# Batch 0 of a Mamba and mixture-of-experts kernel: the side work of TensorE and ScalarE dealt anew over its sixteen steps

## The chip, the core and the metric

One NeuronCore of a Trainium2 chip runs the whole program. Its engines work from queues of their own and meet only at semaphores: TensorE (PE, with its weight loads as PEld), VectorE (DVE), ScalarE (ACT), GpSimd (POOL), and SyncE (SP), which here issues DMAs. The metric is the time of one execution on the device in microseconds, lower is better; the median of three runs of the kernel before is 659.77 us.

## What is computed

Eight sequences of 512 rows of 128 features go through a layer norm, and from its output through two branches that are added to x: a Mamba block and a mixture of 8 experts of which each row takes 2.

```python
xn = _layernorm(x)
# Mamba: 256 channels, 16 states
xn_ = xn * rsqrt(mean(xn * xn) + eps) * norm_w
x_s, z = split(xn_ @ in_proj_w.T)
u = silu(conv1d(x_s, conv_w, taps=4) + conv_b)
dt_raw, B, C = split(u @ x_proj_w.T)
delta = softplus(dt_raw @ dt_proj_w.T + dt_proj_b)
h_t = exp(delta_t * A) * h_(t-1) + delta_t * u_t * B_t     # for 16 states
y = (h * C).sum(states) + u * D_param
mamba = (y * silu(z)) @ out_proj_w.T + xn
# experts
top_w, sel = top_k(xn @ w_router.T, 2);  gates = softmax(top_w)
moe = sum_e gates[:, e] * ((silu(xn @ w_gate[e]) * (xn @ w_up[e])) @ w_down[e])
return x + mamba + moe
```

## The kernel before

The sequences are the batches 0 to 7 (`b`), the 16 states of the recurrence are the steps of a batch (`k`), and a batch has two halves `hf` of 128 channels. A step scans its state over all 512 positions at once: `scan` (L1070) on DVE, one instruction for each half, from the decay exp(delta A) and the input delta u B. Then `product` (L1087) multiplies the states with the row C, and PE adds it up over the steps in PSUM, transposed on the way (`accumulate`, L1354: eight 128x128 transposes). Each engine has a list of its own, written out by hand: `step0(k)` for the steps of batch 0, `step(b, k)` for those of the others, and which side work goes into which step stands in small tables. Nothing reorders it.

In batch 0 the input of the scan is not made by POOL, which is still busy with the norm, but by ScalarE and PE. `scaled(k)` (L518) scales the transposed delta u with the column B on ScalarE into `dbu`, four instructions; `dbu_turn(0, k, hf)` (L1317) turns it back into a PSUM bank, four transposes for each half. Three banks take turns, so the turn for half m waits until the product two halves before is done (`freed`, `p_rdy`). ScalarE also writes the decays (`decay`, L490) two steps ahead. From batch 1 on POOL makes the input (`scaled`, L883, two 128x512 products a step), and the decays are written into the PSUM bank (`decay_bank`, L502).

Beside this batch 0 carries side work:
- **Turned rows and logits.** `rows_normed` (L996, DVE, tensor_scalar from `x_sb` to `xh_all`, four for each group) makes the normed rows, the last two groups in steps of `LATE_ROWS`. `xh_turn(b)` (L1271) turns them on PE, `xh_out(b)` (L461) copies them to `xhT` on ScalarE, `logits(b)` (L1277) is the router's product, four matmuls 8 columns wide.
- **Choices.** When all logits are there, `choices` (L1005 to L1014) picks two experts on DVE in twelve operations. POOL adds the choices (`sel`), PE counts them (`totals`, `ranking`), ScalarE copies (`totals_out`, `ranks_out`), POOL works out the slots (L836 to L855, signals `lohi_rdy`), and DVE's `one_hots` (L1034, L1035, L1037; two groups a step by `HOT_STEP` in steps 12 to 15) with PE's `inverse` (L1304) invert the map. POOL's L861 to L864 make `texp`, the expert of each tile, on one partition; SP waits for it to load weights. In step 15 DVE makes the gates (`weights`, L1020 to L1024).
- **Front of batches 1 and 2.** `conv(c, hf, taps)` (L1386, two matmuls of 512 columns for each tap in fp32 passes, two taps a step), `half_tanh` (L690, L693) on ScalarE and `unit` (L1101) on DVE make u; `rows(c)` (PE L1401, ScalarE L699) makes B, C and dt, which SP stores (`rows_out`) and loads spread over all partitions (`rows_in`, `out_rows_in`); `steps_mm` (L1409), `magnitudes`, `vanishing`, `rounded`, `corrected`, `logarithm` (ScalarE) and `raise_sum`, `correct`, `softplus`, `input_scale` (POOL, L415, L421, L436, L444, one 128x512 operation for each half) make delta and delta u.
- **z and skip.** `z_mm` (L1437) and `z_gate` (ScalarE L647, DVE L1184) in the steps of `z_step(0)`; `skip` (L1366) adds u D into the sum, in `SKIPPED0`.
- **keep** (L1263) is a matmul whose result nobody reads.

POOL's own list before the choices is the weights' scaling (L787 to L791), 32 tensor_scalars of the norm (L795) and eight additions x + xn (L809, 128x512). SP's list has `rows_out(1)` ahead of `out_rows_in(0, 3)`, the C rows that products 12 to 15 read.

## Time and profile before

| | us |
|---|---|
| median of 3 runs | 659.77 (659.0 to 662.25) |
| the profiled execution | 662.08 |
| its span, first to last instruction | 660.2 |
| DVE busy | 604.0 (91%) |
| PE busy / ScalarE / POOL | 565.8 / 423.4 / 502.6 |
| batch 0's steps on DVE | 35.57 to 137.08 |

The page gives the share of each engine; the shares are means over stages with different limits, so batch 0 is read for itself: the table of stretches for how busy DVE is, the list of waits for what it waits on, and the timelines of DVE, PE, ScalarE and POOL side by side. A timeline row gives the start, the time from the start of the first to the end of the last of its instructions, engine, line, operation, tiles, and in brackets the idle time before it with what ended it. Durations of matmuls include their latency; the distance between starts is what they hold PE for.

### The profile page before, as it was taken

Reading aid. Unit: us, or ns where it says so; the run is one execution under the profiler, and the core shown is the slowest. Engines: PE = TensorE matmul, PEld = TensorE weight load, DVE = VectorE, ACT = ScalarE, POOL = GpSimd, SP = SyncE. Lnnn points to the kernel's source line nnn. Section 1 sums busy time; section 2 is a strip of 40 time slices with the busy share of each in tenths; the row PEclk is TensorE's granted clock in tenths of the full one; section 3 lists DMA queues with packets and bytes.
Section 4 is the critical chain, followed back from the end, with each engine's and each line's share of the span. In section 5 each row is a group of like instructions: output and inputs, shape, how many; then the busy total and the mean of one; then the engine's idle time right before and its main releaser. Section 6 shows DMA issues by size and latency. Waiting matters only on the chain.

```text
span 660.2 us, 11497 instructions
## 1 busy us (share of the span) xinstructions
PE 565.8 (86%) x3582; PEld 437.6 (66%) x3582; DVE 604.0 (91%) x867; ACT 423.4 (64%) x839; POOL 502.6 (76%) x504
## 2 busy tenths in 40 slices
PE   5979889888898989999898989989897876779788
PEld 2368576646777777777777777777774554657654
DVE  6966979999999999999999999999998886979957
ACT  1694797137656766657656766657654689469681
POOL 5794059459898798978998798978878869748770
PEclk9868989979999999999999999999998997899979
DMA  7450321425786986888787886888743343223621
GB/s 228 152 181 0 106 91 64 136 72 190 256 264 227 288 268 226 270 272 293 253 256 238 250 294 233 263 274 295 267 146 144 108 163 124 80 80 108 188 65 32
DMA packets 59198, 122.90 MB, mean 186 GB/s; under 512 B 8314, under 2 KB 39426, under 8 KB 52098
## 3 DMA queue, kind: packets, MB, share of 16 engines
q1 hardware_dynamic: 53922, 112.39, 50.3%
q0 software_dynamic: 4496, 9.45, 5.3%
q8 instruction: 29, 0.48, 0.3%
q10 hardware_dynamic: 720, 0.33, 0.3%
q14 instruction: 31, 0.25, 0.1%
HBM read 112.70 MB, written 9.44 MB: 185 GB/s over the span
## 4 chain that ended last, share of the span: by engine, by line
PE 46%; DVE 21%; ACT 15%; issue 10%; POOL 6%; DMA 1%; DVEq 0%; ACTq 0%; POOLq 0%
DVE bank L1070 9%; PE bank L1480 6%; PE bank L1386 6%; PE bank L1354 6%; DVE h_sb L1087 5%; PE bank L1494 4%; ACT dbu L518 4%; POOL dbu L883 4%; PE bank L1488 4%; PE bank L1317 3%; ACT da L490 3%; PE bank L1409 2%; PE bank L1401 2%; PE bank L1455 2%; PE bank L1263 2%
## 5 line engine op out<-in xcount | busy, mean ns | idle before, releaser
L883 POOL TENSOR_TENSOR dbu<-du,xn_all 128x512 f32<-128x512 f32 x178 | 223.2, 1276 | 57.3 <-DVE bank L1070 57.0
L1070 DVE TENSOR_TENSOR_SCAN bank<-bank,dbu 128x512 f32<-128x512 f32 x176 | 214.8, 1224 | 3.9 <-ACT bank L502 3.9
L502 ACT ACTIVATE bank<-delta,a_sb 128x512 f32<-128x512 f32 x176 | 121.4, 691 | 108.2 <-DVE h_sb L1087 106.2
L1087 DVE TENSOR_TENSOR h_sb<-bank,xh_all 128x512 f32<-128x512 f32 x240 | 159.8, 680 | 1.2
L1354 PE MATMUL bank<-id_sb,h_sb 128*128 128x128 f32 x992 | 134.7, 281 | 12.4 <-DVE h_sb L1087 10.9
L1354 PEld LDWEIGHTS bank<-id_sb,h_sb 128*128 128x128 f32 x992 | 116.2, 146 | 26.3 <-DVE h_sb L1087 19.3
L1070 DVE TENSOR_TENSOR_SCAN bank<-da,bank 128x512 f32<-128x512 f32 x76 | 90.5, 1218 | 34.0 <-PE bank L1317 33.8
L1480 PEld LDWEIGHTS bank<-wd_sb,hid 117*128 117x128 f32 (+1 forms) x432 | 55.2, 191 | 54.4 <-DVE hid L1121 31.3
L1480 PE MATMUL bank<-wd_sb,hid 117*128 117x128 f32 (+1 forms) x432 | 64.1, 284 | 24.5 <-ACT xT L661 12.5
L870 POOL DMA_INDIRECT xs<-xn_rows,src x72 | 70.6, 981 | 11.3 <-issue 7.4
L1317 PE MATMUL bank<-id_sb,dbu 128*128 128x128 f32 x304 | 52.1, 299 | 30.8 <-ACT dbu L518 27.5
L1317 PEld LDWEIGHTS bank<-id_sb,dbu 128*128 128x128 f32 x304 | 38.9, 154 | 50.3 <-ACT dbu L518 32.5
L518 ACT ACTIVATE dbu<-du_t,bc_sb 128x256 f32<-128x256 f32 x152 | 64.4, 496 | 0.4 <-PE bank L1317 0.3
L1488 PE MATMUL bank<-xT,wgu_sb 128*118 128x128 f32 x432 | 59.8, 275 | 4.1 <-DVE ga L1114 4.1
L1386 PE MATMUL bank<-xhT,wk_sb 128*128 128x512 f32 x128 | 61.4, 608 | 0.7 <-ACT xhT L461 0.7
L1494 PE MATMUL bank<-xT,wgu_sb 128*118 128x128 f32 x432 | 59.1, 272 | 0.0
L1488 PEld LDWEIGHTS bank<-xT,wgu_sb 128*118 128x118 f32 x432 | 52.3, 182 | 6.2 <-issue 6.1
L912 POOL DMA_INDIRECT xhT<-y_slots,slot x48 | 46.6, 971 | 12.1 <-issue 10.5
L490 ACT ACTIVATE da<-delta,a_sb 128x512 f32<-128x512 f32 x80 | 53.1, 711 | 2.9 <-DVE bank L1070 2.7
L1494 PEld LDWEIGHTS bank<-xT,wgu_sb 128*118 128x118 f32 x432 | 52.7, 182 | 0.5 <-issue 0.5
L667 ACT ACTIVATE th<-bank 118x384 f32<-118x384 f32 x72 | 34.7, 483 | 18.4 <-PE bank L1488 18.4
L1263 PE MATMUL bank<-wk_sb,id_sb 128*128 128x256 f32 (+3 forms) x108 | 46.3, 520 | 0.0
...
## 6 DMA issues: line engine op xcount, KB each, us to landing
xh_all<-b_rows SPq DMA_DIRECT2D x30, 1024.0 KB, 6.5
xn_all<-b_rows SPq DMA_DIRECT2D x25, 1024.0 KB, 7.3
...
```

Of the source, the lines that this page charges most:

```text
L490: nc.scalar.activation(da_of(n)[:, hf, :], delta[b % 2][:, hf, :], ACT.Exp, scale=a_sb[:, hf, k:k + 1]).then_inc(s["da_rdy"], 1)
L502: nc.scalar.activation(bank_of(b, m)[:, :], delta[b % 2][:, hf, :], ACT.Exp, scale=a_sb[:, hf, k:k + 1]).then_inc(s["da_rdy"], 1)
L518: last = nc.scalar.activation(dbuT[k % 2][:, t, :], duT[:, t, :], ACT.Copy, scale=bc_sb[q][:, t, k:k + 1])
L883: nc.gpsimd.tensor_tensor(dbu[k % 2][:, hf, :], du[b % 2][:, hf, :], b_ring[c % 2][:, k % CH, :], ALU.mult).then_inc(s["dbu_p"], 1)
L1070: nc.vector.tensor_tensor_scan(at, da_of(n)[:, hf, :] if n in IN_SBUF else at, inp, 0.0, ALU.mult, ALU.add).then_inc(s["h_rdy"], 1)
L1087: nc.vector.tensor_tensor(h_sb[k % 2][:, hf, :], bank_of(b, 2 * k + hf)[:, :], row, ALU.mult).then_inc(s["p_rdy"], 1)
L1317: last = nc.tensor.transpose(at[:, t * P:(t + 1) * P], dbuT[k % 2][:, t, hf * P:(hf + 1) * P], id_sb[:, :])
L1354: last = MM(HT[i][:, t % 2, hf * P:(hf + 1) * P], h_sb[k % 2][:, hf, t * P:(t + 1) * P], id_sb[:, :], is_transpose=True, start=(k == 0 and ...
L1386: last = MM(at[:, :], wk_sb[:, tap, hf * P:(hf + 1) * P], xhT[:, c, tap:tap + T], start=(tap == taps[0] if c == 0 else tap == 0), stop=(ta ...
L1480: last = MM(XD[:, P:P + H], hid[j % 2][0:FN[c], c * P:(c + 1) * P], wd_sb[j % NW][0:FN[c], c, :], start=(c == 0), stop=(c == NF - 1))
L1488: last = MM(GB[0:FW, c * P:(c + 1) * P], wgu_sb[j % NW][:, c * FS:c * FS + FW], xT[j % 2][:, :], start=True, stop=True)
L1494: last = MM(UB[0:FW, c * P:(c + 1) * P], wgu_sb[j % NW][:, F + c * FS:F + c * FS + FW], xT[j % 2][:, :], start=True, stop=True)
```

## The change

Only batch 0 and what leads to it are changed, and no operation of the reference. All row numbers here are of the kernel before.

PE: logits 1 and 2 go ahead of step 0 with three keeps; the other turns and logits go to the even steps 0 to 6 and 8. The conv of batch 1's second half goes to steps 3 and 5, batch 2's to 7, 8 and 13, 14. `totals` and `ranking` come in step 9, `rows(1)` in step 10, `steps_mm` in 11 and 12. Keeps stand in steps 0, 1, 12 and 15 alone. ScalarE copies turned rows one step after PE turned them, `rows(1)` comes in step 11, the magnitudes in 12 and 13, the logarithm in 13, `half_tanh(2, 1)` in step 15 behind `decay_bank`. DVE: late rows in steps 0 and 2, choices in step 8, units in 1, 6, 9 and 15. POOL: the eight operations of batch 1's front come last. Waits of conv and rows are changed to fit.

```diff
-    TURNED, SKIPPED, SKIPPED0 = 11, (1, 2), (7, 8)
+    TURNED, SKIPPED, SKIPPED0 = 11, (1, 2), (8, 10)
-        LOGITS_AT = {0: (1, 2), 1: (3,), 2: (4,), 3: (5,), 5: (6,), 6: (7,)}
-        LATE_ROWS = {0: (24, 28), 4: (28, 32)}
+        LOGITS_AT = {0: 3, 2: 4, 4: 5, 6: 6, 8: 7}
+        LATE_ROWS = {0: (24, 28), 2: (28, 32)}
...
-            return {0: 4, 2: 5, 3: 6, 5: 7}.get(k)
+            return {0: 4, 2: 5, 4: 6, 6: 7}.get(k)
...
-            return {13: 1, 15: 0} if b == 0 else {8: 1, 10: 0} if b == 6 else {4: 1, 6: 0}
+            return {12: 1, 14: 0} if b == 0 else {8: 1, 10: 0} if b == 6 else {4: 1, 6: 0}
...
+                if k == 10:
+                    ranks_out()
...
-                if b_turn(k) is not None:
-                    xh_out(b_turn(k))
-                if k in (0, 4):
-                    half_tanh(1, k // 4)
-                if k == 6:
+                if b_turn(k - 1) is not None:
+                    xh_out(b_turn(k - 1))
+                if k in (0, 6):
+                    half_tanh(1, k // 6)
+                if k == 9:
+                    half_tanh(2, 0)
+                    totals_out()
+                if k == 10:
+                    spread_choices()
+                if k == 11:
                     rows(1)
...
+                if k == 15:
+                    half_tanh(2, 1)
...
-                if k == 7:
+                if k == 8:
                     choices()
-                if k in (11, 14):
-                    unit(2, k // 14)
+                if k in (9, 15):
+                    unit(2, k // 15)
...
-                if k < 6:
+                if k < 2:
                     keep(LGB[:, 2 * C - 2 * H + 2 * E:])
-                if k >= 12:
+                if k == 12 or k == 15:
                     keep(MAP[:, P:], k == 12)
                     keep(MAP[:, P:], False)
```

On PE, steps 2 and 3 of batch 0, from the first turn of step 2's second half (each `L1317` row is one half, `L1354` the accumulation). Before:

```order
L1317 MATMUL bank<-id_sb,dbu 128x128 x4
L1354 MATMUL bank<-id_sb,h_sb 128x128 x8
L1317 MATMUL bank<-id_sb,dbu 128x128 x4
L1386 MATMUL bank<-xhT,wk_sb 128x512 x2
L1271 MATMUL bank<-id_sb,xh_all 128x128 x4
L1277 MATMUL bank<-wr_sb,xhT 128x8 x4
L1263 MATMUL bank<-wk_sb,id_sb 128x240
```

And now (step 2, then step 3; a conv pair is now L1388):

```order
L1317 MATMUL bank<-id_sb,dbu 128x128 x4
L1354 MATMUL bank<-id_sb,h_sb 128x128 x8
L1317 MATMUL bank<-id_sb,dbu 128x128 x4
L1277 MATMUL bank<-wr_sb,xhT 128x8 x4
L1271 MATMUL bank<-id_sb,xh_all 128x128 x4
L1317 MATMUL bank<-id_sb,dbu 128x128 x4
L1354 MATMUL bank<-id_sb,h_sb 128x128 x8
L1317 MATMUL bank<-id_sb,dbu 128x128 x4
L1388 MATMUL bank<-xhT,wk_sb 128x512 x2
```

A step's side work is now either a turn with logits or a conv pair, and the keep is gone.

On POOL, from the last operations of the slots to the first products of batch 1 (L421 corrects, L436 makes delta, L444 delta u, L415 raises the sum). Before:

```order
L855 CAST hi<-hi 128x64
L421 TENSOR_TENSOR sp_m<-sp_m,sp_e 128x512 x2
L436 TENSOR_TENSOR delta<-sp_d,sp_m 128x512 x2
L444 TENSOR_TENSOR du<-delta,u_sb 128x512 x2
L861 TENSOR_SCALAR wgu_sb<-lanes_sb,ends 1x72 x8
L822 TENSOR_TENSOR wgu_sb<-wgu_sb 1x288
L823 TENSOR_TENSOR wgu_sb<-wgu_sb 1x144
L824 TENSOR_TENSOR tsum<-wgu_sb 1x72
L864 TENSOR_SCALAR texp<-tsum 1x72
L883 TENSOR_TENSOR dbu<-du,xn_all 128x512 x6
```

And now:

```order
L856 CAST hi<-hi 128x64
L858 TENSOR_SCALAR wgu_sb<-lanes_sb,ends 1x72 x8
L825 TENSOR_TENSOR wgu_sb<-wgu_sb 1x288
L826 TENSOR_TENSOR wgu_sb<-wgu_sb 1x144
L827 TENSOR_TENSOR tsum<-wgu_sb 1x72
L861 TENSOR_SCALAR texp<-tsum 1x72
L415 TENSOR_TENSOR sp_m<-sp_m,sp_y 128x512 x2
L421 TENSOR_TENSOR sp_m<-sp_m,sp_e 128x512 x2
L436 TENSOR_TENSOR delta<-sp_d,sp_m 128x512 x2
L444 TENSOR_TENSOR du<-delta,u_sb 128x512 x2
L883 TENSOR_TENSOR dbu<-du,xn_all 128x512 x6
```

The eight 128x512 operations of batch 1's front stand in one row behind `texp`; the two raises stood ahead of the slots before.

On ScalarE, the end of step 14 and step 15 of batch 0 (with the semaphores waited for). Before:

```order
L690 ACTIVATE u_sb<-bank,cbh_sb 128x512 [waits p_rdy,xc_mm]
L693 ACTIVATE u_sb<-u_sb,sign_sb 128x512 [waits x_th]
L647 ACTIVATE zs_sb<-bank 128x512 [waits z_mm]
L502 ACTIVATE bank<-delta,a_sb 128x512 [waits delta_rdy,p_rdy] x2
L655 ACTIVATE g_sb<-bank 128x512 [waits acc_mm] x2
```

And now (the first row ends step 14):

```order
L650 ACTIVATE zs_sb<-bank 128x512 [waits z_mm]
L502 ACTIVATE bank<-delta,a_sb 128x512 [waits delta_rdy,p_rdy]
L693 ACTIVATE u_sb<-bank,cbh_sb 128x512 [waits p_rdy,xc_mm]
L696 ACTIVATE u_sb<-u_sb,sign_sb 128x512 [waits x_th]
L502 ACTIVATE bank<-delta,a_sb 128x512 [waits delta_rdy,p_rdy]
L658 ACTIVATE g_sb<-bank 128x512 [waits acc_mm] x2
```

The two instructions of `half_tanh(2, 1)` stand behind the first `decay_bank` of batch 1.

## Rows read from the trace of the kernel before

**Rows 1.** Stretches: from:to, length; busy us of each engine, PEclk, DMA, GB/s

```profile
35.57:137.08 101.51, 85.73 (x470) 66.84 (x470) 84.69 (x122) 66.69 (x127) 55.99 (x76) 0.86 0.28 96
...
160.00:300.00 140.00, 125.99 (x932) 106.10 (x933) 138.83 (x193) 90.86 (x184) 122.99 (x106) 1.00 0.77 254
```

**Rows 2.** Waits of DVE in batch 0: who, on whom, us in total, times, longest

```profile
DVE bank L1070 <- PE bank L1317: 15.8, 9, 4.7
```

**Rows 3.** Timeline of DVE: start, us, line, operation, [idle before]

```profile
47.27 1.23 DVE L1070 TENSOR_TENSOR_SCAN bank<-da,bank 128x512 f32<-128x512 f32 x1 [4.69 <-PE bank L1317]
...
66.70 1.11 DVE L996 TENSOR_SCALAR xh_all<-x_sb,mean,both 128x128 f32<-128x128 f32 x4
...
76.22 2.33 DVE L1070 TENSOR_TENSOR_SCAN bank<-da,bank 128x512 f32<-128x512 f32 x2
78.46 1.27 DVE L1087 TENSOR_TENSOR h_sb<-bank,u_sb 128x512 f32<-128x512 f32 x2
79.64 0.42 DVE L1005 COPY wgu_sb<-bank 128x256 f32<-128x256 f32 x1
```

**Rows 4.** Timeline of PE: own work, side work at two levels of the clock

```profile
40.12 1.12 PE L1317 MATMUL bank<-id_sb,dbu 128*128 128x128 f32 x4 [4.78 <-ACT dbu L518]
...
48.66 1.06 PE L1317 MATMUL bank<-id_sb,dbu 128*128 128x128 f32 x4
...
57.17 0.96 PE L1277 MATMUL bank<-wr_sb,xhT 128*128 128x8 f32 x8
...
60.22 1.88 PE L1386 MATMUL bank<-xhT,wk_sb 128*128 128x512 f32 x4
...
69.56 1.91 PE L1401 MATMUL bank<-u_sb,xp_sb 128*40 128x512 f32 x4
...
140.18 3.45 PE L1401 MATMUL bank<-u_sb,xp_sb 128*40 128x512 f32 x4
```

**Rows 5.** Stretches of one microsecond, the granted clock third from the end

```profile
38.00:39.00 1.00, 0.00 (x0) 0.00 (x0) 1.00 (x3) 0.97 (x3) 1.00 (x2) 0.50 0.78 238
...
54.00:55.00 1.00, 1.00 (x8) 1.00 (x7) 1.00 (x3) 0.00 (x0) 1.00 (x2) 0.72 0.00 0
```

**Rows 6.** Timeline of ScalarE: second half of a half_tanh, first decays of batch 1

```profile
102.71 0.72 ACT L693 ACTIVATE u_sb<-u_sb,sign_sb 128x512 f32<-128x512 f32 x1
...
131.06 1.30 ACT L502 ACTIVATE bank<-delta,a_sb 128x512 f32<-128x512 f32 x2 [7.80 <-DVE h_sb L1087]
```

**Rows 7.** Timeline of DVE: one-hots and gates beside POOL and alone

```profile
107.55 2.68 DVE L1034 TENSOR_TENSOR lo_oh<-lanes_sb,lo 128x1024 f16<-128x1024 f16 x1
...
132.13 0.94 DVE L1020 TENSOR_SCALAR p<-p 128x32 f32<-128x32 f32 x1
...
133.71 0.18 DVE L1023 TENSOR_SCALAR p<-p 128x32 f32<-128x32 f32 x1
...
134.14 0.69 DVE L1034 TENSOR_TENSOR lo_oh<-lanes_sb,lo 128x1024 f16<-128x1024 f16 x1
```

**Rows 8.** Timeline of POOL: seven of the eight additions

```profile
48.25 8.64 POOL L809 TENSOR_TENSOR x_sb<-x_sb,xn_all 128x512 f32<-128x512 f32 x7
```

**Rows 9.** Timeline of POOL and of DVE in the first 10 us

```profile
7.12 2.77 POOL L790 TENSOR_TENSOR wk_sb<-wk_sb,g_sb 128x256 f32<-128x256 f32 x4
...
7.29 0.58 DVE L984 TENSOR_SCALAR mean<-mean 128x4 f32<-128x4 f32 x1
...
9.27 0.65 DVE L989 TENSOR_SCALAR both<-both 128x8 f32<-128x8 f32 x1
```

**Rows 10.** Timeline of POOL: start of the slots, last of the front, end of the counts

```profile
92.20 0.20 POOL L836 TENSOR_SCALAR tiles<-wgu_sb 128x8 f32<-128x8 f32 x1 [3.27 <-ACT wgu_sb L471]
...
107.16 2.52 POOL L444 TENSOR_TENSOR du<-delta,u_sb 128x512 f32<-128x512 f32 x2
...
119.00 0.71 POOL L864 TENSOR_SCALAR texp<-tsum 1x72 int32<-1x72 f32 x1
```

**Rows 11.** DMA issues of the page: KB each, median us from issue to landing

```profile
xh_all<-b_rows SPq DMA_DIRECT2D x30, 1024.0 KB, 6.5
```

More of the change, by code:

```diff
@@ L829, in _ @@
             nc.gpsimd.tensor_tensor(kk[:, :], kk[:, :], irms[:, :], ALU.mult).then_inc(s["top_rdy"], 1)
-            for hf in range(NH):
-                raise_sum(pool, nc.gpsimd, 1, hf)
             pool.wait_ge(s["rk_out"], 1)
@@ L1505, in step0 @@
                     inverse(g)
-                if k in (2, 3):
-                    conv(1, 1, (2 * k - 4, 2 * k - 3))
-                if k == 5:
-                    rows(1)
+                if k == 9:
+                    totals()
+                    ranking()
+                if k in LOGITS_AT:
+                    logits(LOGITS_AT[k])
+                if b_turn(k) is not None:
+                    xh_turn(b_turn(k))
+                if k in (3, 5):
+                    conv(1, 1, (k - 3, k - 2))
+                if k in (7, 8):
+                    conv(2, 0, (2 * k - 14, 2 * k - 13))
+                if k == 10:
+                    rows(1)
+                if k in (11, 12):
+                    steps_mm(1, k - 11)
+                if k in (13, 14):
+                    conv(2, 1, (2 * k - 26, 2 * k - 25))
+                if k + 1 in z_step(0):
+                    z_mm(0, k)
                 if k in SKIPPED0:
                     skip(0, (SKIPPED0.index(k),))
-                if k == 8:
-                    totals()
-                    ranking()
-                if k in (9, 10):
-                    conv(2, 0, (2 * k - 18, 2 * k - 17))
-                if k in (12, 13):
-                    conv(2, 1, (2 * k - 24, 2 * k - 23))
-                if k + 1 in z_step(0):
-                    z_mm(0, k)
-                if b_turn(k) is not None:
-                    xh_turn(b_turn(k))
-                for i in LOGITS_AT.get(k, ()):
-                    logits(i)
-                if k == 7:
-                    steps_mm(1, 0)
-                    steps_mm(1, 1)
-                if k < 6:
+                if k < 2:
                     keep(LGB[:, 2 * C - 2 * H + 2 * E:])
-                if k >= 12:
+                if k == 12 or k == 15:
                     keep(MAP[:, P:], k == 12)
@@ L1615, in _ @@
             input_turn(0, 0)
+            logits(1)
+            keep(LGB[:, 2 * C - 2 * H + 2 * E:])
+            logits(2)
+            keep(LGB[:, 2 * C - 2 * H + 2 * E:])
+            keep(LGB[:, 2 * C - 2 * H + 2 * E:])
             for k in range(S):
```

35 lines of the change are left out of this document (15 added, 20 removed).

## Prediction, made before the changed kernel ran

> **What bounds the kernel now.** I read the table of stretches first. In batch 0's sixteen steps, 35.57 to 137.08 us, DVE is busy 84.69 of 101.51 us, and in 160 to 300 us 138.83 of 140 [rows 1]. So behind batch 0 DVE is full: whatever batch 0 ends earlier or later comes out at the end of the kernel nearly whole. The list of waits says what DVE's idle time in batch 0 is: 15.8 us in nine waits of scans on the transposes of `dbu_turn` (L1317) [rows 2], and 0.3 us on ScalarE at the start, which stays. DVE's timeline shows the pattern: at 47.27 a scan had waited 4.69 us; from 76.22 on nothing waits, and a full step is 2.24 us from scans to products and 1.18 us of products, 3.42 us in all [rows 3].
>
> The waits stand where PE's side work is longer than DVE's step. At full clock PE's own part of a step is about 1.8 us: each half of `dbu_turn` 0.44, `accumulate` 0.9. Two taps of `conv` add 1.72, one `logits` 0.82 [rows 4], `xh_turn` is as long as a half of `dbu_turn`, `keep` 0.5. Steps 2 and 3 now carry conv, turn, logits and keep together, 5.3 us. At the lower level all of it doubles: the transposes at 48.66 take 0.85 to the next start, and `rows` takes 3.4 us at 140.18 against 1.85 at 69.56 [rows 4]. PE had stood idle for 4.78 us before 40.12 [rows 4]; the granted clock is half from 38 us and rises at 54.7 [rows 5].
>
> **What the change takes away.** Odd steps now have a conv pair (1.8 + 1.7 = 3.5 us), even steps a turn and a logits (3.1 us): both about DVE's 3.42. Walking the steps with these lengths, scans of steps 2 to 9 find their transposes ready if the clock is high. What stays of the waits:
> - Step 1. Its first transposes are released by ScalarE's scaling at 40.12 as before; high clock leaves 0.5 us of the wait. The second half comes behind a logits, a turn and a keep: 0.95 us wait at 2.4 GHz, 2.65 at 1.2. PE's idle time shrinks from 4.78 to about 1.6 us, since logits 1 and 2 and three keeps (3.1 us) now fill it. I take the middle, 1.8.
> - Step 11. Step 10 has `rows` (1.85) and one skip (0.9) beside 1.8: 4.5 us, 0.1 us wait at the high level. But PE idles some 3 us while DVE makes the choices (twelve operations of DVE from 79.64, 5.37 us [rows 3]), and low clock makes rows 3.4 us: 2 to 3.5 us. Taken 2.6.
> - Step 15, a new wait. `unit(2,1)` now stands behind product 15, and its input is made by ScalarE behind `decay_bank(16,0)`, which itself waits for product(15,0). Decay 0.61 after 0.71, tanh 0.70, half 0.72: 2.77 us after that product's start [rows 6], while DVE is there after 1.18. Wait 1.6; the weights and the last one-hots queue behind it.
>
> Of 16.1 us idle, 0.3 + 0.5 + 1.8 + 2.6 + 1.6 = 6.8 stay: **-9.3 us**.
>
> **What it moves under POOL.** DVE operations with both inputs in SBUF, or tensor_scalar between SBUF tiles, get longer beside POOL's tensor_tensor. Two such places go: the one-hot at 107.55 took 2.68 us against 0.69 at 134.14, ending 0.58 behind POOL's last `du` product, and L1020 took 0.94 at 132.13 where its like at 133.71 took 0.18 [rows 7]. In the new order the count chain of 1-partition operations lies beside the first one-hots (-2.0), and POOL's product is over at L1020 (-0.75): **-2.75 us**.
>
> Two places come. First, `rows_normed(28, 32)` goes from step 4 (66.70, 1.11 us, POOL idle) [rows 3] to step 2, at 49 to 51 us, and POOL adds seven 128x512 tiles without a gap from 48.25 to 56.89 [rows 8]. How does DVE fare against such a chain? The early stretch shows tensor_scalars and tensor_tensors of a few elements against four back-to-back POOL products: each ends some 0.05 us after the POOL operation that it began in (7.29 takes 0.58, 9.27 takes 0.65, base 0.18; two more between them) [rows 9]. So one DVE operation per POOL operation: four at 0.6 + 3 x 1.2: **+4.2 us** (0.5 if all four slip through together, 6.6 if none until 56.89). PE then starves for 2.3 to 4 us; if the clock falls, the next two steps' side work (5.9 us against 3.42) costs 1.35 + 1.0. Between 0 and 2.35, taken **+1.5**.
>
> Second, the front of batch 1. Before, POOL's eight 128x512 operations were two by two: two raises at 86, then six from 102.18, the last two at 107.16 [rows 10], mostly beside scans and products that read PSUM. Now all eight come behind `texp`. Clock them from the end of the choices. DVE: steps 9 to 12 of 3.42, a unit 0.66, a z gate 0.6, the wait 2.6: first one-hots at 17.5; 2.94 long, then step 13: second pair at 23.9. POOL: sum of choices, totals, ranking, copy 4.6, slots 10.0 (from 92.20 to the chain of six), counts 10.1 (from that chain's end at 109.65 to the end of `texp`, 119.71) [rows 10]: the chain of eight starts at 24.7 and runs 8 x 1.25 = 10.0 us, to 34.7. It meets the second pair after about two of its six operations. The nearest row is the one-hot at 107.55: it waited past the end of one POOL product (108.4) to the end of the next, though it had asked 0.85 us before. If a gapless chain keeps it out, four operations (1.9 us, and 0.2 between) follow 34.7: 13.0 us for the pair against 3.8: **+9.2**. By one for one: 4 x 1.24, and 1.4 more in step 14's pair: +6.1. By slipping in once: +2.5. I take the row of the same operation, 9.2.
>
> The Trainium skill (SBUF — State Buffer, "Who interferes with whom") says that GpSimd and such a VectorE operation hold the pair of ports for one whole instruction. By that sentence alone the second term would be 6.1 and the time 659.5; the wait at 107.55 went past one instruction's end.
>
> **Costed at nothing.** The rows that product 12 reads (c_in, 1 MB) are now issued after ScalarE's rows(1) in step 11, not step 6; such a transfer lands 6.5 us after its issue in the median [rows 11], and 7 us of DVE work lie between. `lohi` is there at 14.6, asked at 17.5. `scaled(15)` waits for the logarithm and its table, over 9 us ahead of scan 15. POOL's product for batch 1 has some 10 us in hand without the stalls. `texp` and expert weights come earlier. Each wait that ends late would show as a DVE wait.
>
> **Sum.** -9.3 - 2.75 + 4.2 + 1.5 + 9.2 = **+2.85 us**. The profiled span of 660.2 would be 663.1 (its execution 662.08 would be 664.9, 1.9 us outside the span); on the median of 659.77, which is 2.3 below that execution, it gives **662.6**.
>
> **Rivals.**
> - One for one throughout: the HOT pair at +6.1, so -0.25: 659.5. For it: four early rows; against: 107.55.
> - DVE hardly kept out: rows 0.5, no clock loss, pair +2.5: -9.05, 650.7. For it: chains on POOL need not be as gapless once DVE asks; against: every row where both met.
> - Slower, one mechanism: POOL's chain of adds at 48.25 keeps `rows_normed` out until 56.89, 6.6 us, with the clock loss full, 2.35: +6.1, 665.9. It decides once the rows wait past the second POOL add.
> - Slower by the clock: two keeps instead of six in steps 0 to 5, so PE stays at 1.2 GHz through steps 2 to 8; each costs 1.9 to 2.8 us, so four such steps beyond the forecast give +9: 672.
> - The change does what it says and nothing is given back elsewhere: no row for it; it is the second rival.
>
> **How the numbers follow.** Chances: forecast 0.33, one for one 0.22, hardly kept out 0.2, adds keep it out 0.19, clock 0.06. The range takes in 650.7 with nothing below, and 665.9 with a microsecond of scatter: 650.5 to 667. A measurement tells apart about 0.5%, 3.3 us: faster means below 656.5, slower above 663.1. The second rival is faster, with some tail of the first: 0.24. Forecast (its centre just inside, split 0.17 same, 0.16 slower) and one for one (0.17 same, 0.02 slower): same 0.35; slower 0.41.
>
> **What would show it.** DVE's waits on L1317 in batch 0: about 5 us, none in steps 2 to 9 but one or two behind the rows. The four L996 near 50 us: 5 us in all if right, 1.1 if not, 7 if kept out. The third one-hot of L1034, some 24 us behind the choices: 9 to 10 us long, or split over L1034, L1035 and L1037 at 1.2 more each. A wait of 1.6 us before the L1101 of step 15. The lower clock at 78 to 88 us. If L996 and L1034 keep their lengths, the forecast is wrong by its two largest terms.

## The result, and the profile of the changed kernel

The changed kernel takes 663.11 us in the median of 20 runs (661.3 to 666.25), the kernel before 660.1 (658.04 to 662.75, 20 runs): a ratio of 1.0043, interval 1.003 to 1.0057. It is slower by a small step that is clear of noise. The profiled execution of the new kernel is its slowest, 666.25 us with a span of 664.5, and has the lowest mean granted clock of the twenty (0.943; the others 0.948 to 0.956), so its waits on PE may be longer than is typical; that of before had 662.08 us and a span of 660.2.

Line numbers on ScalarE, PE and GpSimd are shifted by a few (adds L809 are now L812, `half_tanh` L693 is L696, `conv` L1388); those of VectorE used here are the same. The first row answers to the first of [rows 1]: batch 0's steps, from the first scan to batch 1's.

```profile
35.40:138.67 103.27, 86.28 (x459) 68.74 (x459) 91.40 (x122) 65.18 (x124) 57.44 (x77) 0.81 0.27 94
```

Batch 0 got 1.76 us longer (101.51 before), and in it DVE is busy 6.7 us more with the same 122 instructions: the waits did go down, but operations got longer. The list of DVE's waits in that stretch (who, on whom, us in total, times, longest), beside [rows 2]:

```profile
DVE bank L1070 <- PE bank L1317: 9.0, 7, 2.9
DVE u_sb L1101 <- ACT u_sb L696: 1.5, 1, 1.5
DVE lo_oh L1034 <- PE bank L1304: 0.4, 1, 0.4
```

15.8 us in nine waits became 9.0 in seven, and two small ones are new. DVE's timeline shows where, and which operations got longer:

```profile
42.13 1.23 DVE L1070 TENSOR_TENSOR_SCAN bank<-da,bank 128x512 f32<-128x512 f32 x1 [2.10 <-PE bank L1317]
46.23 1.23 DVE L1070 TENSOR_TENSOR_SCAN bank<-da,bank 128x512 f32<-128x512 f32 x1 [2.88 <-PE bank L1317]
...
52.64 5.52 DVE L996 TENSOR_SCALAR xh_all<-x_sb,mean,both 128x128 f32<-128x128 f32 x4
58.08 2.33 DVE L1070 TENSOR_TENSOR_SCAN bank<-da,bank 128x512 f32<-128x512 f32 x2
...
68.19 1.23 DVE L1070 TENSOR_TENSOR_SCAN bank<-da,bank 128x512 f32<-128x512 f32 x1 [1.44 <-PE bank L1317]
...
98.07 1.23 DVE L1070 TENSOR_TENSOR_SCAN bank<-da,bank 128x512 f32<-128x512 f32 x1 [1.14 <-PE bank L1317]
...
104.84 0.68 DVE L1034 TENSOR_TENSOR lo_oh<-lanes_sb,lo 128x1024 f16<-128x1024 f16 x1
...
111.68 0.74 DVE L1034 TENSOR_TENSOR lo_oh<-lanes_sb,lo 128x1024 f16<-128x1024 f16 x1 [0.41 <-PE bank L1304]
112.34 1.52 DVE L1035 TENSOR_TENSOR hi_val<-lanes_sb,hi 128x576 f16<-128x576 f16 x1
113.90 1.41 DVE L1037 TENSOR_TENSOR hi_val<-hi_val,lanes_sb 128x576 f16<-128x576 f16 x1
115.24 1.76 DVE L1034 TENSOR_TENSOR lo_oh<-lanes_sb,lo 128x1024 f16<-128x1024 f16 x1
116.92 1.54 DVE L1035 TENSOR_TENSOR hi_val<-lanes_sb,hi 128x576 f16<-128x576 f16 x1
118.50 1.40 DVE L1037 TENSOR_TENSOR hi_val<-hi_val,lanes_sb 128x576 f16<-128x576 f16 x1
119.82 2.33 DVE L1070 TENSOR_TENSOR_SCAN bank<-da,bank 128x512 f32<-128x512 f32 x2
...
133.82 0.75 DVE L1101 SCALAR_TENSOR_TENSOR u_sb<-bank,cb_sb,u_sb 128x512 f32<-128x512 f32 x1 [1.53 <-ACT u_sb L696]
134.49 0.17 DVE L1020 TENSOR_SCALAR p<-p 128x32 f32<-128x32 f32 x1
```

The four L996 took 5.52 us where they took 1.11 in step 4 [rows 3]. The one-hots of step 12 (from 104.84) are at base length; the pair of step 13, 111.68 to 119.82, took 8.14 where the kernel before needed 3.8. GpSimd's timeline beside these two places, against [rows 8] and [rows 10]:

```profile
48.65 8.66 POOL L812 TENSOR_TENSOR x_sb<-x_sb,xn_all 128x512 f32<-128x512 f32 x7
58.24 1.26 POOL L812 TENSOR_TENSOR x_sb<-x_sb,xn_all 128x512 f32<-128x512 f32 x1 [0.93 <-DVE xh_all L996]
...
112.11 2.88 POOL L415 TENSOR_TENSOR sp_m<-sp_m,sp_y 128x512 f32<-128x512 f32 x2
114.96 3.18 POOL L421 TENSOR_TENSOR sp_m<-sp_m,sp_e 128x512 f32<-128x512 f32 x2
118.11 2.96 POOL L436 TENSOR_TENSOR delta<-sp_d,sp_m 128x512 f32<-128x512 f32 x2
121.03 2.49 POOL L444 TENSOR_TENSOR du<-delta,u_sb 128x512 f32<-128x512 f32 x2
```

One of the four L996 makes them long. The view of that tile gives shortest, median and longest in ns:

```profile
L996 DVE TENSOR_SCALAR xh_all<-x_sb,mean,both x4: 333/334/4755, 52.6 to 57.8; 128x128 f32<-128x128 f32 x4
```

Three took 0.33 us, one 4.76. The last started at 57.8, and two of 0.33 fit between it and 57.3, so the long one was the first, from 52.64 to 57.39; GpSimd's row of seven additions ended at 48.65 + 8.66 = 57.31. The row ends there because its eighth addition waits for these very rows (`[0.93 <-DVE xh_all L996]`): the hold was over only when GpSimd itself stopped to wait. At the other place no operation is held that long: each one-hot operation got in once per GpSimd operation, about 1.0 us later than alone, and the GpSimd operations got longer by what they let in (two in 2.9 to 3.2 us in place of 2.5).

The table puts it together: the start of the first product (L1087) of each step, in us, read from DVE's timelines. It also holds the experiments that ran on the same chip as each other (e1 to e4) and four from chips on which the kernel before is slower; step 16 is batch 1's first.

| step | 1 | 2 | 3 | 4 | 7 | 8 | 12 | 13 | 14 | 15 | 16 |
|---|---|---|---|---|---|---|---|---|---|---|---|
| before | 48.4 | 54.3 | 60.3 | 65.5 | 78.5 | 87.2 | 106.4 | 114.7 | 122.5 | 130.3 | 138.4 |
| after | 47.4 | 51.5 | 60.3 | 63.7 | 77.5 | 80.9 | 103.1 | 110.0 | 122.1 | 131.0 | 140.0 |
| e1 rows in step 4 | 42.0 | 46.1 | 49.6 | 53.0 | 69.2 | 72.6 | 93.1 | 100.1 | 111.1 | 120.8 | 129.8 |
| e2 adds after the rows | 42.2 | 46.2 | 51.1 | 54.6 | 66.4 | 69.8 | 91.9 | 99.0 | 110.5 | 119.4 | 128.4 |
| e3 front in gaps | 42.1 | 46.2 | 59.7 | 63.1 | 75.0 | 78.4 | 101.7 | 108.7 | 115.0 | 123.0 | 135.3 |
| e4 no early keeps | 46.5 | 50.6 | 60.3 | 63.7 | 75.3 | 78.7 | 100.9 | 107.8 | 119.3 | 128.3 | 137.3 |
| e6 unit last | 42.0 | 46.1 | 59.6 | 63.0 | 74.8 | 78.2 | 98.7 | 105.7 | 116.7 | 126.4 | 134.6 |
| e9 halved rows | 43.9 | 48.0 | 61.3 | 64.7 | 78.8 | 82.2 | 104.4 | 111.4 | 120.1 | 129.5 | 138.5 |
| e10 adds apart | 43.8 | 47.9 | 56.2 | 59.6 | 71.2 | 74.7 | 98.0 | 105.0 | 116.5 | 125.5 | 134.5 |
| e12 halved front | 41.9 | 46.0 | 50.9 | 54.3 | 66.1 | 69.5 | 91.9 | 98.8 | 107.6 | 117.0 | 124.3 |

(The choices stand between steps 7 and 8 before and between 8 and 9 since, which is 5.4 us of step 8's lead.) Between the kernel before and after, the lead of 2.8 us at step 2 is zero at step 3, and the lead of 4.7 at step 13 is 0.4 at step 14. Both losses stand where DVE works beside GpSimd.

### The profile page after: what moved, and what is told of

It is laid out like the page before. It is cut to its first block, busy times and chain, and to the rows that moved or that the text cites. A ratio compares the mean times of both kernels' runs of the same rounds, so it can differ in the third digit from the quotient of the medians.

```text
span 664.5 us, 11478 instructions
## 1 busy us (share of the span) xinstructions
PE 566.1 (85%) x3572; PEld 440.0 (66%) x3572; DVE 610.7 (92%) x867; ACT 424.2 (64%) x839; POOL 504.2 (76%) x504
## 4 chain that ended last, share of the span: by engine, by line
PE 44%; DVE 24%; issue 12%; ACT 12%; POOL 5%; DMA 3%; SPq 0%; DVEq 0%; ACTq 0%
DVE bank L1070 10%; PE bank L1482 6%; PE bank L1354 6%; DVE h_sb L1087 5%; PE bank L1388 5%; PE bank L1496 4%; PE bank L1490 4%; PE bank L1317 3%; POOL dbu L883 3%; PE bank L1457 2%; ACT dbu L518 2%; ACT da L490 2%; PE bank L1263 2%; PE bank L1411 2%; PE bank L1403 2%
## 5 line engine op out<-in xcount | busy, mean ns | idle before, releaser
L1087 DVE TENSOR_TENSOR h_sb<-bank,xh_all 128x512 f32<-128x512 f32 x240 | 158.8, 675 | 1.2
L1354 PE MATMUL bank<-id_sb,h_sb 128*128 128x128 f32 x992 | 135.6, 282 | 14.0 <-DVE h_sb L1087 12.6
L1354 PEld LDWEIGHTS bank<-id_sb,h_sb 128*128 128x128 f32 x992 | 117.1, 146 | 28.1 <-DVE h_sb L1087 21.3
L870 POOL DMA_INDIRECT xs<-xn_rows,src x72 | 70.8, 983 | 11.4 <-issue 8.3
L1317 PE MATMUL bank<-id_sb,dbu 128*128 128x128 f32 x304 | 53.3, 304 | 26.7 <-ACT dbu L518 19.2
L1317 PEld LDWEIGHTS bank<-id_sb,dbu 128*128 128x128 f32 x304 | 40.9, 158 | 45.4 <-ACT dbu L518 23.4
L1388 PE MATMUL bank<-xhT,wk_sb 128*128 128x512 f32 x128 | 61.2, 606 | 0.7 <-ACT xhT L461 0.7
L1263 PE MATMUL bank<-wk_sb,id_sb 128*128 128x256 f32 (+3 forms) x98 | 43.1, 531 | 0.0
```

What stands on the lines that cost most here:

```text
L870: nc.gpsimd.indirect_dma_start(xs[i][:, :], None, xn_rows, bass.IndirectOffsetOnAxis(ap=src[:, j:j + 1], axis=0)).then_inc(s[f"xs_in{i}"], 16)
L1087: nc.vector.tensor_tensor(h_sb[k % 2][:, hf, :], bank_of(b, 2 * k + hf)[:, :], row, ALU.mult).then_inc(s["p_rdy"], 1)
L1317: last = nc.tensor.transpose(at[:, t * P:(t + 1) * P], dbuT[k % 2][:, t, hf * P:(hf + 1) * P], id_sb[:, :])
L1354: last = MM(HT[i][:, t % 2, hf * P:(hf + 1) * P], h_sb[k % 2][:, hf, t * P:(t + 1) * P], id_sb[:, :], is_transpose=True, start=(k == 0 and ...
L1388: last = MM(at[:, :], wk_sb[:, tap, hf * P:(hf + 1) * P], xhT[:, c, tap:tap + T], start=(tap == taps[0] if c == 0 else tap == 0), stop=(ta ...
```

## The experiments

Runs of one group share a chip and the runs of the kernel before on it; these stood at 660.3, 665.1 and 666.7 us, so ratios are compared.

**e1: rows where they stood.**

```
-        LATE_ROWS = {0: (24, 28), 2: (28, 32)}
+        LATE_ROWS = {0: (24, 28), 4: (28, 32)}
```

> The changed kernel with one number undone: the last group of normed rows is made in step 4 again, not in step 2. Theory (the rows stand beside POOL's gapless additions and get in once for each): the four tensor_scalars fall from 5.52 us to about 1.1, PE no longer idles 5.1 us in step 4 and keeps its high clock, so the waits of 1.44 and 0.51 us in steps 5 and 6 go too: 6.3 us off the changed kernel, 656.8 against 660.1 before, ratio 0.995. Rival (the rows are slow in themselves, or ScalarE and PE would have made DVE wait there anyway): L996 stays at 5 us or a wait on L1317 of the same size takes its place, and the time stays at 663, ratio 1.004.

656.06 us in the median, ratio 0.9944 (0.9919 to 0.9969); the change as it was has 1.0043. But the rows did not get short. In this execution the clock was high and DVE did not wait in step 1; it came to step 4 at 54.17, and met the end of the same additions. DVE's timeline and the tile's view:

```profile
54.17 3.82 DVE L996 TENSOR_SCALAR xh_all<-x_sb,mean,both 128x128 f32<-128x128 f32 x4
```

```profile
L996 DVE TENSOR_SCALAR xh_all<-x_sb,mean,both x4: 334/336/3050, 54.2 to 57.7; 128x128 f32<-128x128 f32 x4
```

Again one operation lasts until the seventh addition ends. The ratio is what was expected (0.995), but not for the reason given: the four took 3.82 us, not 1.1. What was gained is that two steps of work were done ahead of them, while GpSimd added.

**e2: the additions behind the rows.**

```
+            pool.wait_ge(s["xh_w"], NT)
             for b in range(NB):
                 pool.wait_ge(s["xh_w"], b * TT + TT)
```

> The changed kernel with the rows left in step 2, but POOL's eight additions wait for the last of them. It tells POOL's chain from the place of the rows. Theory: with POOL silent the four L996 take 1.1 us in step 2, and the time is that of the kernel with the rows in step 4, about 657, ratio 0.995. Rival (the place): L996 stays at 5 us, 663. The additions then end near 62 us; POOL has nothing else to do until the choices, so they cost nothing.

653.12 us, ratio 0.9894 (0.9862 to 0.9926): 1.5% below the change as it was, from one wait on GpSimd. DVE's timeline, and then GpSimd's:

```profile
47.42 1.57 DVE L997 TENSOR_SCALAR xh_all<-x_sb,mean,both 128x128 f32<-128x128 f32 x4
```

```profile
49.08 9.90 POOL L813 TENSOR_TENSOR x_sb<-x_sb,xn_all 128x512 f32<-128x512 f32 x8 [0.41 <-DVE xh_all L997]
```

The additions started 0.4 us later than in the kernel after, all eight ran through, and nothing waited for them. The gain is larger than expected (0.9894 for 0.995), since nothing is held to 57 us any more. One more row of this timeline matters below: a small tensor_tensor met the same additions and was not held to their end.

```profile
56.13 0.44 DVE L1142 TENSOR_TENSOR irms<-irms,both 128x32 f32<-128x32 f32 x1
```

It takes 0.19 us where GpSimd is idle. By step 8 e2 is 11.1 us ahead of after, and 11.6 at step 16.

**e3: the front of batch 1 in two parts behind the one-hots of steps 13 and 14.**

```
             nc.gpsimd.tensor_scalar(texp[:, 0:NJ], ...).then_inc(s["texp_rdy"], 1)
+            pool.wait_ge(s["hi_rdy"], 4)
             remainder(pool, nc.gpsimd, 1)
+            pool.wait_ge(s["hi_rdy"], 6)
             softplus(pool, nc.gpsimd, 1, 1)
```

> The changed kernel with POOL's eight operations of batch 1's front cut into two chains by waits: raise and correct start when the second pair of one-hots is made, softplus and input scale when the third is. Both chains then lie beside scans and products that read PSUM. Theory (the port, one DVE operation for each POOL operation): the pairs of steps 13 and 14 fall from 8.14 and 4.94 us to about 3.0 each, 7.1 us off the changed kernel: 656.0, ratio 0.994. Rival (batch 1's front now comes too late): DVE waits for dbu L883 or ScalarE for L436 at the start of batch 1, 2 to 5 us, and only 2 to 5 us are gained. Rival (the one-hots are slow because PE's map or their operands are late): lengths stay, 663.

660.39 us, ratio 0.9995 (0.9972 to 1.0017): 0.5% below after, some 3 us where 7.1 were expected. Step 13 to 14 shrank from 12.05 to 6.35 us: against one-hots that meet nothing, the collision cost 5.7 us there. 3.3 us of it came back in step 15, where GpSimd's front and products now ran beside the gates, one by one (DVE's timeline):

```profile
127.77 0.81 DVE L1024 TENSOR_TENSOR p<-p 128x32 f32<-128x32 f32 x1
128.62 1.18 DVE L1025 TENSOR_SCALAR p<-p 128x32 f32<-128x32 f32 x1
129.82 1.18 DVE L1026 TENSOR_SCALAR p<-p 128x32 f32<-128x32 f32 x1
```

Alone these take 0.19, 0.18 and 0.18. So this gate on GpSimd did not take the collision away as a whole; it moved part of it to other operations.

**e4: without the three keeps ahead of step 0.**

```
             logits(1)
-            keep(LGB[:, 2 * C - 2 * H + 2 * E:])
             logits(2)
-            keep(LGB[:, 2 * C - 2 * H + 2 * E:])
-            keep(LGB[:, 2 * C - 2 * H + 2 * E:])
```

> The changed kernel without the three keeps ahead of step 0; logits 1 and 2 stay there. In the changed kernel's trace ScalarE's scaled input is ready at 38.05 us, but PE comes to its turn at 40.96 behind logits and keeps at the low clock. Theory (the early side work itself is late at 1.2 GHz): the first turn comes 2.9 us earlier, at 38.1, and the two waits of step 1 (2.10 and 2.88 us) fall to 2 together; 2.5 to 2.9 us off, 660.4, ratio 1.0005. Rival (the keeps are what lets the clock rise at 48 us): the clock stays low two to three steps longer, the turns of steps 2 and 3 make DVE wait 2 to 4 us more, and the time is the same or up to 2 us longer, ratio 1.003 to 1.007.

662.46 us, ratio 1.0035 (1.0019 to 1.0051): no difference from after. Step 2's product came 0.9 us earlier, the rows took 6.39 in place of 5.52, and step 3's product starts at the same 60.3.

```profile
51.76 6.39 DVE L996 TENSOR_SCALAR xh_all<-x_sb,mean,both 128x128 f32<-128x128 f32 x4
```
 With rows in step 2 and additions in one row, step 3 stands at 59.6 to 60.3 in after, e3, e4 and e6, whether step 2 was at 46.1 or at 51.5. In these kernels the lead up to there is worth nothing.

**e6: the last unit behind the gates and one-hots.**

```
-                if k in (9, 15):
-                    unit(2, k // 15)
+                if k == 9:
+                    unit(2, 0)
...
                 for g in HOT_STEP.get(k, ()):
                     one_hots(g)
+                if k == 15:
+                    unit(2, 1)
```

> The kernel after with unit(2,1) moved behind step 15's gates and last one-hots on VectorE. Theory: the wait of 1.53 us before that unit goes, since ScalarE's half_tanh(2,1) ends over 3 us before VectorE comes to it, and nothing takes its place: 663.1 - 1.5 = 661.6, no wait of VectorE on ScalarE's L696 in step 15, scan (16,0) 1.5 us earlier against the last product of step 15. Rival: VectorE has slack there in another form (GpSimd's products for batch 1, or PE's inverse, come late next), and the time stays at 663.1.

Ratio 1.0024 (1.001 to 1.0039) on a chip where before takes 665.1: 0.2% less than after. The two intervals overlap, so the trace has to carry it: the wait of 1.53 us on L696 is gone and the unit takes 0.74 us at 132.55. But from step 15's product to step 16's it is only 0.9 us less (8.1 for 9.0), because the gates now meet GpSimd's products: L1020 and L1022 take 0.30 and 0.83 us for 0.17 and 0.19. Its PE clock was high in steps 0 and 1 and it waited 0.6 us on L1317 in all of batch 0, not 9.0; still its rows lasted to 57.4. Its clock (third figure from the end), its rows on DVE's timeline, and the tile's view:

```profile
35.00:36.00 1.00, 1.00 (x11) 1.00 (x10) 0.90 (x2) 1.00 (x3) 1.00 (x2) 1.00 1.16 310
...
47.27 10.13 DVE L996 TENSOR_SCALAR xh_all<-x_sb,mean,both 128x128 f32<-128x128 f32 x4
```

```profile
L996 DVE TENSOR_SCALAR xh_all<-x_sb,mean,both x4: 335/532/8970, 47.3 to 57.1; 128x128 f32<-128x128 f32 x4
```

Here the long one was the third, from 48.18 to 57.15. The first two took 0.68 and 0.39 us and were over before the first addition started at 48.47.

**e5: a probe of the two engines alone.** Each cell is written out, for instance:

```
pool:  for each of 8:  nc.gpsimd.tensor_tensor(acc[4 tiles], x_sb[4 tiles], xn_all[4 tiles], ALU.add)
dve:   wait for the first; 4 x nc.vector.tensor_scalar(xh_all[i], xd[i], mean[i], sxh[i], ALU.subtract, ALU.mult)
```

> A kernel of its own that computes nothing of the reference: sixteen cells in a row. In each, GpSimd runs eight 128x512 additions in place, and VectorE waits for the first and then issues four operations. Cells differ in VectorE's operation (tensor_scalar 128x128 with two pointers, as in rows_normed; with constants; the one-hot's tensor_tensor 128x1024 f16; others) and in GpSimd's row (no waits; each behind a wait long satisfied; each behind the addition two before; sixteen of 256 columns); two controls for each engine alone. It is to explain why in the kernel after the first rows_normed operation of step 2 took 4.76 us, to the end of the row of seven additions, while one-hots beside the front of batch 1 took 1.4 to 1.8 each. Theory A, GpSimd's row decides: without waits any VectorE operation that needs the port lasts until the row ends, some 8.6 us for the first and base length for the others (0.33, 0.68); with waits about 1.2 each. Theory B, VectorE's operation decides: the one with pointers is kept out to the end in either row (8.6), the f16 tensor_tensor gets in once for each addition (1.2 to 1.7 each, the additions longer by its 0.45 to 0.68) in either. Theory C, one for one always: four times about 1.2 everywhere, 0.6 where the additions are 256 wide; then the 4.76 us has another cause.

Theory C: GpSimd's row is given up once for each addition in every cell. The small tensor_scalars (128x32) even got in two at a time, one of 1.22 us and one of 0.17. Rows on DVE from three cells: the first cell, the one-hots, and the additions 256 columns wide:

```profile
10.37 1.21 DVE L304 TENSOR_SCALAR xh_all<-xd,mean,sxh 128x128 f32<-128x128 f32 x1 [1.50 <-POOL x_sb L93]
11.50 1.30 DVE L305 TENSOR_SCALAR xh_all<-xd,mean,sxh 128x128 f32<-128x128 f32 x1
...
30.05 1.73 DVE L318 TENSOR_TENSOR lo_oh<-lanes_sb,lo 128x1024 f16<-128x1024 f16 x1 [4.94 <-POOL x_sb L115]
...
114.74 0.76 DVE L378 TENSOR_SCALAR xh_all<-xd,mean,sxh 128x128 f32<-128x128 f32 x1
```

An operation of 0.33 us takes 1.30 beside additions that start every 1.22 us, and 0.76 beside those of half the width. A one-hot operation of 0.68 us takes 1.75 beside additions that now start every 1.67 us. So in the probe each VectorE operation waits for about one GpSimd operation, and waits less when that operation is shorter.

**e8: the same with the tiles, waits and neighbours of the kernel.**

> A second kernel of its own, with the tiles of the kernel after at their addresses, that computes nothing of the reference: eleven cells, each a row of GpSimd operations and beside it rows_normed's tensor_scalars or another kind. In the kernel after and its variants the operation of rows_normed that met the row of seven additions lasted to the end of that row (3.05, 4.76, 5.63 and 8.97 us), yet in the first probe the same operation beside eight such additions got in once for each (1.30 us). Cells: c0 all as in the kernel (three PSUM products of VectorE first, two satisfied waits ahead of each addition, rows read from x_sb, an eighth addition that waits for the rows); c1 without the eighth; c2 rows read from another tile; c3 additions without waits; c4 one-hots; c5 small tensor_scalars; c6 without the products ahead; c7 twelve row operations that begin ahead of the additions; c8 out-of-place products and one-hots; c9 with ScalarE busy; c10 with DMAs running. Theory A, VectorE's three PSUM operations right ahead are what the first probe lacked: c1 to c5 have one operation that lasts to the end of the row (5 to 6 us), c6 has four of 1.3. Theory B, it is x_sb, read by one and written by the other: c2 alone is free of it. Theory C, two waits ahead of each addition: c3 alone is free. Theory D, ScalarE or DMAs: c9 or c10 alone show it. If none does, the cause of the long hold stays open.

None of the theories: no cell showed a long hold; the longest rows_normed operation of all cells took 1.32 us. The cell with everything as in the kernel, on DVE:

```profile
17.62 0.59 DVE L628 TENSOR_SCALAR xh_all<-x_sb,mean,both 128x128 f32<-128x128 f32 x1
18.13 1.30 DVE L629 TENSOR_SCALAR xh_all<-x_sb,mean,both 128x128 f32<-128x128 f32 x1
```

**e10: the additions apart.**

```
                                         xn_all[:, b * TT:(b + 1) * TT, :], ALU.add).then_inc(s["acc_w"], 1)
+                pool.wait_ge(s["acc_w"], b + 1)
```

> The kernel after with each of GpSimd's eight additions waiting for the one before it to be complete, so that the row of additions has a short gap behind each. Theory, the row keeps rows_normed out because it has no gap: the operations of rows_normed then last at most 1.3 us each, and whatever comes first is over by 52.6 when VectorE comes early, so that the four take at most 5.2 us and step 3 starts by 53 to 57 in place of 58.1; the time falls by 1 to 4 us, to 659 to 662. Rival: gaps are not what counts; one of the four lasts to the end of the seventh addition (57.3 or later) as before, 663.

Ratio 0.9926 (0.99 to 0.9951), 1.2% below after, which is more than the 1 to 4 us expected. The tile's view:

```profile
L997 DVE TENSOR_SCALAR xh_all<-x_sb,mean,both x4: 903/1424/1440, 49.1 to 52.6; 128x128 f32<-128x128 f32 x4
```

No operation is held to the end of the row; the four take 4.95 us, from 49.11 to 54.06, and step 3's product stands at 56.2. GpSimd's additions started 1.36 us apart in place of 1.23, 10.73 us in all. With a gap behind each addition VectorE gets in once for each.

**e11: another operation for the rows**, scalar_tensor_tensor in place of tensor_scalar.

```
+                    if n0 == 28:
+                        nc.vector.scalar_tensor_tensor(xh_all[:, n, :], x_sb[:, n, :], mean[:, n:n + 1],
+                                                       sxh[:, n:n + 1].to_broadcast([P, H]), ALU.subtract, ALU.mult)...
```

> The kernel after with rows_normed(28,32) as scalar_tensor_tensor (mean as a pointer, the scale as a broadcast row) in place of tensor_scalar with two pointers; same result, same place. Alone such an operation takes some 0.2 to 0.35 us. Theory A, the kind of VectorE's operation decides: it gets in behind each addition, at most 1.35 us each, since a small tensor_tensor beside the same additions in an earlier run took 0.45. Theory B, it is the place (what the other engines and the DMAs do there) and not the kind: one of the four lasts to the end of the seventh addition, near 57.3 us, as the tensor_scalar did.

Theory B: a scalar_tensor_tensor of the same size is held like the tensor_scalar. This kernel ran once (671.16 us), so only its trace is used.

```profile
L997 DVE SCALAR_TENSOR_TENSOR xh_all<-x_sb,mean,both x4: 339/339/8331, 48.6 to 57.4; 128x128 f32<-128x128 f32 x4
```

**e9: every long operation of GpSimd in two halves.**

```
-                nc.gpsimd.tensor_tensor(acc[:, b * TT:(b + 1) * TT, :], x_sb[...], xn_all[...], ALU.add).then_inc(s["acc_w"], 1)
+                for n in (b * TT, b * TT + 2):
+                    last = nc.gpsimd.tensor_tensor(acc[:, n:n + 2, :], x_sb[:, n:n + 2, :], xn_all[:, n:n + 2, :], ALU.add)
+                last.then_inc(s["acc_w"], 1)
```

The same was done to `raise_sum`, `correct`, `softplus` and `input_scale` of batch 1.

> The kernel after with each 128x512 operation of GpSimd's row of additions and of batch 1's front written as two of 256 columns, nothing else. Theory, one VectorE operation for each GpSimd operation: beside the front each one-hot operation waits about half as long (0.72 us in place of 1.26 for a GpSimd operation), so the pair of step 13 takes 8.1 - 6 x 0.5 = some 5 us, the time falls by 2 to 4 us, to 659 to 661. For the rows of step 2 two answers are open: if they too go one for one, four operations of 0.76; if GpSimd's row of additions keeps them out as it did (one operation of 4.8 to 9 us), one long operation to its end, which is now a microsecond later, and three of 0.33. Rival: what keeps VectorE out is not bound to the single GpSimd operation, and halving them changes neither place: 663 or, by the longer rows of GpSimd, 664.

Ratio 1.0001 (0.9967 to 1.0036), 0.4% below after. The two intervals overlap, so the time alone does not show a gain. The trace has both halves of the answer: the rows are held to the end as before, and the one-hots of step 13 take 5.3 us for the pair where they took 8.14:

```profile
L1004 DVE TENSOR_SCALAR xh_all<-x_sb,mean,both x4: 334/335/9169, 49.2 to 58.8; 128x128 f32<-128x128 f32 x4
```

```profile
113.15 0.98 DVE L1043 TENSOR_TENSOR hi_val<-lanes_sb,hi 128x576 f16<-128x576 f16 x1
114.17 0.86 DVE L1045 TENSOR_TENSOR hi_val<-hi_val,lanes_sb 128x576 f16<-128x576 f16 x1
114.96 1.22 DVE L1042 TENSOR_TENSOR lo_oh<-lanes_sb,lo 128x1024 f16<-128x1024 f16 x1
```

Each is 0.4 to 0.5 us longer than alone where it was 1.0 longer. Step 14's pair now met more of the row (5.4 against 4.94), since GpSimd's row of the front got longer (14.3 us for 11.4).

**e7: additions behind the rows, gates in step 10, unit last.**

```
+            pool.wait_ge(s["xh_w"], NT)
...
+                if k == 10:
+                    weights()
```

> The kernel after with three edits: GpSimd's eight additions wait for rows_normed(28,32) (as in the run before that gave 653.1), the gates (L1020 to L1024, some 1.1 us) go from step 15 to behind product (10,1), where VectorE waited 1.9 us for step 11's transposes, and unit(2,1) goes behind the last one-hots. Theory: of the 653.1 us, 1.5 go with the wait before the unit, and 1.1 since the gates fill a wait: 650.5; VectorE's wait in step 11 falls from 1.9 to about 0.8; L1034 to L1037 in step 13 and 14 still take 8 and 5 us. Rival: PE sets the pace from step 10 to step 14 (steps_mm, z_mm and conv side work), so that the waits of step 11 and 12 stay and the gates bring nothing: 651.6 with the wait for the unit gone, or 653.1 without.

Ratio 0.9882 (0.9846 to 0.9917), where e2 had 0.9894 (0.9862 to 0.9926): a gain over e2, of which 2.6 us were expected, is not shown by the ratios. In the trace the wait of step 11 did go, but the gates took 1.97 us in step 10 (84.28 to 86.25, beside GpSimd's slots; 1.25 in step 15 of e10, where GpSimd was idle), so that step 11's product stands at 88.5 against 88.1 in e2. The unit's 1.5 us are there: batch 1 starts at 126.7 against 128.4.

**e12: e7 with the front of batch 1 in halves** (the second edit of e9).

> The version that has all that the runs so far support: additions behind rows_normed(28,32), gates in step 10, unit(2,1) last in step 15, and the eight operations of batch 1's front on GpSimd written as sixteen of 256 columns. Theory, one VectorE operation for each GpSimd operation: against the run with the first three edits (0.988 of the kernel before) the one-hots of steps 13 and 14 lose some 3 to 4 us less, so 0.982 to 0.984 of before. Rival: GpSimd's row gets longer by the overhead of eight more operations (0.1 us each) and meets more of the one-hots, or the loss for each operation stays: 0.988.

656.69 us where before takes 666.72 on this chip: ratio 0.9829 (0.9802 to 0.9856), the lowest of all, 1.7% ahead of before and, by the ratios, 2.1% ahead of after. Its interval still overlaps a little with e7's, so the halves' own share rests on the trace. Step 13 to 14 takes 8.8 us against 11.5 in e2, and batch 1 starts at 124.3.

## Why the prediction came out right, step by step

662.6 was forecast and 663.1 measured: +3.0 us against the runs of before beside it, where the sum was +2.85. That the two agree so closely is in part luck. The waits taken away and the second one-hots were each off by about 3 us, in opposite directions; the rows in step 2 had the right size by the wrong mechanism; and what stands behind batch 0 had been put at nothing.

- **Waits taken away, -9.3 in the forecast.** The first term was too large. Steps 2 to 4 and 7 to 9 have no wait, as forecast; all waits together went from 16.1 us to 10.9, so -5.2, with those of the low clock (below) among them. Where the term failed is step 1, 2.3 forecast and 4.98 measured. I had taken its first transposes to be released by ScalarE at 40.12 as before. ScalarE's input was ready at 38.1 already (it now writes `decay(0)` ahead of the columns), and PE came late from its own list: the logits and keeps put ahead of step 0 ran at half clock in that execution and ended at 41. ScalarE, PE and the clock (third figure from the end):

```profile
36.39 1.70 ACT L518 ACTIVATE dbu<-du_t,bc_sb 128x256 f32<-128x256 f32 x4
...
39.22 1.95 PE L1263 MATMUL bank<-wk_sb,id_sb 128*128 128x240 f32 x4
40.96 1.06 PE L1317 MATMUL bank<-id_sb,dbu 128*128 128x128 f32 x4
...
35.00:36.00 1.00, 1.00 (x8) 1.00 (x6) 0.90 (x2) 1.00 (x3) 1.00 (x2) 0.50 1.22 386
```

These waits are not what the kernel's time hangs on while the rows are held: e3 and e6 had none of them and still reach step 3's product at 59.7 and 59.6. In the executions of e1, e2, e3 and e6 the clock is high there. The prediction also says that nothing waits from 76.22 on, which holds for two steps only: the kernel before waited 2.35, 0.93 and 0.82 us at 92.0, 96.7 and 101.0, and steps 10 to 12 of the new one still wait 2.13.
- **First one-hots and L1020, -2.75.** 0.68 us at 104.84 for 2.68, 0.17 at 134.49 for 0.94: right, -2.8.
- **Rows in step 2, +4.2.** Measured +4.4, and right by accident. The step that failed is "one DVE operation per POOL operation". It came from [rows 9] and does not hold here: one operation was kept out to the end of the additions (after, e1, e3, e4, e6, e9, e11). That is the mechanism of the rival at 665.9. Its price is set by when VectorE arrives: 4.4 us on arrival at 52.6, 9.0 on arrival at 47.3 (e6: 10.13 for 1.11). Since it ends at about 57.4 either way, what it costs is the whole lead up to step 3. The term was also too high for its own mechanism: 0.6 + 3 x 1.2 = 4.2 is how long the four would last, and less the 1.11 us that they take anyway it adds 3.1; in e10, where they do get in one for one, it adds 4.95 - 1.11 = 3.8.
- **Low clock after it, +1.5.** PE was idle for 5.11 us before 61.13, the granted clock was 0.50 at 60, and the waits behind are 1.44 and 0.51: 1.95. Within the 0 to 2.35 that were given.

```profile
60.00:61.00 1.00, 0.00 (x0) 0.00 (x0) 1.00 (x3) 0.61 (x2) 0.00 (x0) 0.50 0.00 0
...
61.13 1.09 PE L1317 MATMUL bank<-id_sb,dbu 128*128 128x128 f32 x4 [5.11 <-DVE h_sb L1087]
```

- **Step 11 and step 15.** 2.13 us in steps 10 to 12 for 2.6, 1.53 for 1.6. Both right in size. The items costed at nothing in batch 0 brought one wait of 0.4 us, on PE's `inverse` (L1304).
- **Chances.** The parts given for "slower" (0.16, 0.02, 0.19 and 0.06) add up to 0.43, not 0.41.
- **Sum.** -5.2 - 2.8 + 4.4 + 5.6 = +2.0, and batch 0 is 1.76 longer. The forecast had the low clock as a term of its own; with it, its waits are -9.3 + 1.5 = -7.8, where -5.2 was measured, so it took 2.6 too much away; and its +9.2 for the second one-hots added 3.6 too much. Behind batch 0 the profiled execution lost another 2.5: DVE's waits on L1317 there are 20.6 us, 18.0 before. From step 16's product to the end it took 521.8 us before, 524.5 after, and 521.9, 523.2, 522.0 and 523.3 in e1 to e4, whose code there is the same, so I count it as scatter between executions. Of the median's +3.0, batch 0's 1.8 leaves 1.2 for which no cause is shown.

e2 shows what the change is worth without the first collision: the kernel is then 9.8 us faster than after (1.0043 - 0.9894 of 660) and 1.1% faster than before. So the new order of PE's side work does gain time; most of it was lost again where VectorE stood waiting behind GpSimd.

What stays open is why GpSimd's row of additions is not given up to these operations inside the kernel and is in both probes. A tensor_scalar and a scalar_tensor_tensor are held alike (e11), and so is one beside additions of half the length (e9). The tiles, the waits ahead of each addition, the products ahead, a busy ScalarE and DMAs, each set beside the row alone, do not bring the hold about (e8); whether they are needed for it is not shown. A gap ends it (e10). Nor is the row closed to everything in the kernel: the tensor_tensor of 128x32 in e2 (L1142, 0.44 us at 56.13) was let in with more additions to come, and so was its like in e7 and e12. What the size of the VectorE operation does, and what the other engines do all together, was not tried.
